# Cross-attention and routed experts on one core: the opening of the attention stage re-cut, and the row statistics spread over six units

## What is computed

```
q = (layernorm(x) @ w_q.T + b_q) * 32**-0.5
k = ctx @ w_k.T + b_k ;  v = ctx @ w_v.T + b_v
scores = q.k per head + attn_bias ; masked keys get -max
out = softmax(scores) @ v
x = x + out @ w_out.T + b_out
y = layernorm(x)
# 32 prototypes: distance to each, softmax, best two kept and renormalised
x = x + sum over the two best experts: A[e] @ (B[e] @ y) + bias[e]
```

## Time and profile before

| | |
|---|---|
| median of 3 runs | 939.32 us (937.33 to 940.16) |
| the profiled execution, its own time | 940.71 us |
| its span, first to last instruction | 939.0 us |
| TensorE busy in the span | 874.2 us (93%) |
| VectorE, ScalarE, GpSimd busy | 621.2, 499.9, 200.4 us |
| mean granted TensorE clock | 0.978 of full speed |

### The profile page before, as it was taken

How to read it: one execution, slowest core, us unless ns; L and a number is a source line. 1 busy time by engine, 2 the same in 40 slices (tenths; PEclk the granted TensorE clock), 3 DMA queues, 4 the chain that set the end, 5 groups by cost and what they waited for, 6 DMA issues and landing times. The chain is left out here.

```text
span 939.0 us, 20884 instructions
## 1 busy us (share of the span) xinstructions
PE 874.2 (93%) x8016; PEld 761.9 (81%) x8016; DVE 621.2 (66%) x1452; ACT 499.9 (53%) x1061; POOL 200.4 (21%) x245
## 2 busy tenths in 40 slices
PE   7789999999999999999999999999989778999996
PEld 6678987898889788978987898889777567878884
DVE  5646675667667766766676667666677465666663
ACT  4226655565556565656655565556577334444431
POOL 1251022002201121220022002210084213333200
PEclk9889999999999999999999999999999979999999
DMA  7795654554565556655654554475565211222101
GB/s 247 220 221 132 161 142 119 143 155 119 137 166 150 134 142 146 166 131 136 152 150 120 143 154 120 104 177 139 131 163 121 67 40 40 62 65 68 59 20 39
DMA packets 79402, 119.77 MB, mean 128 GB/s; under 512 B 8469, under 2 KB 58749, under 8 KB 79314
## 3 DMA queue, kind: packets, MB, share of 16 engines
q1 hardware_dynamic: 76818, 109.91, 45.9%
q0 software_dynamic: 2496, 8.65, 3.0%
HBM read 79.25 MB, written 39.28 MB: 126 GB/s over the span
## 5 line engine op out<-in xcount | busy, mean ns | idle before, releaser
L568 ACT ACTIVATE score_sb<-score_sb,neg_max 112x750 f32<-112x750 f32 x256 | 236.0, 922 | 94.4 <-DVE neg_max L696 93.6
L696 DVE CUSTOM_DVE_ANT_0 score_sb<-score_ps,neg_bias 112x750 f32<-112x750 f32 x256 | 239.5, 935 | 65.3 <-PE score_ps L858 63.4
L867 PE MATMUL prob_ps<-ident,score_sb 112*125 112x112 f32 x1536 | 254.7, 275 | 18.9 <-ACT score_sb L568 8.5
L867 PEld LDWEIGHTS prob_ps<-ident,score_sb 112*125 112x125 f32 x1536 | 226.5, 189 | 51.5 <-issue 13.3
L577 ACT ACTIVATE probs_sb<-prob_ps 125x336 f32<-125x336 f32 x256 | 114.8, 449 | 181.5 <-PE prob_ps L867 179.9
L706 DVE COPY probs_sb<-prob_ps 125x336 f32<-125x336 f32 x256 | 129.6, 506 | 120.5 <-PE prob_ps L867 118.3
L465 POOL COPY rsum_wide<-rsum 112x256 f32<-112x256 f32 x32 | 12.8, 399 | 460.6 <-DVE rsum L715 460.5
L854 PE MATMUL score_ps<-k_st,q_st 97*112 97x512 f32 x256 | 108.4, 424 | 0.0
L813 PE MATMUL acc<-ctx_hi,w_hi 128*128 128x376 f32 (+1 forms) x256 | 93.9, 367 | 7.5 <-DVE ctx_lo L731 6.7
L813 PE MATMUL acc<-ctx_hi,w_lo 128*128 128x376 f32 (+1 forms) x256 | 91.8, 358 | 0.0
L813 PE MATMUL acc<-ctx_lo,w_hi 128*128 128x376 f32 (+1 forms) x256 | 91.5, 357 | 0.0
(11 more groups left out here) (163 smaller groups left out, 1510.8 us busy)
## 6 DMA issues: line engine op xcount, KB each, us to landing
k_st<-k_parts SPq DMA_DIRECT2D x96, 375.0 KB
q_st<-q_parts SPq DMA_DIRECT2D x96, 112.0 KB
ctx_raw<-in_ctx_t SPq DMA_DIRECT2D x14, 752.0 KB, 7.0
k_parts<-k_hi SPq DMA_DIRECT2D x30, 188.0 KB, 1.9
k_parts<-k_lo SPq DMA_DIRECT2D x30, 188.0 KB, 2.3
k_parts<-k_hi SPq DMA_DIRECT2D x30, 187.0 KB, 2.9
k_parts<-k_lo SPq DMA_DIRECT2D x30, 187.0 KB, 4.3
xb<-in_x SPq DMA_DIRECT2D x8, 448.0 KB, 4.1
```

The source lines that it names most:

```text
L568: nc.scalar.activation(scores[:, w % NSC, :], scores[:, w % NSC, :], ACT.Exp, bias=neg_max[:, w % UB:w % UB + 1], scale=-1.0, accum_out=su ...
L696: nc.vector.tensor_tensor_reduce(out=scores[:, w % NSC, :], in0=score_ps[:, at:at + S], in1=neg_bias[:, w // HG % TC, :], scale=1.0, scala ...
L867: last = nc.tensor.transpose(prob_ps[j][0:SW, s * TW:(s + 1) * TW], scores[:, w % NSC, (BT * j + s) * SW:(BT * j + s + 1) * SW], ident[0:T ...
```

## The change

- **Query weights.** GpSimd's three operations are gone. The weights come in four DMAs of a quarter each. ScalarE makes the high part of each quarter straight from the stage with scale -SCALE (`high_queries`, behind the high evictions of tiles 3, 4, 4 and 5), VectorE the low part by one scalar_tensor_tensor (`low_queries`, behind the low evictions of tiles 4, 5, 5 and 6).
- **Value weights.** The quarters' high parts stand together (one before the eviction of tile 7, three behind it), the low parts behind tiles 7 (three) and 8 (one). Before, they stood one by one behind tiles 6 to 9.
- **Statistics of batch 0:** `newton` and `normalise` stand behind tile 3 (before: tile 4). Batch 1: statistics behind tile 12 (before: 10), normalisation behind 13 (before: 12). `turn_x(c)` waits only for its own half.
- **Bias:** negated by VectorE behind tiles 10 and 11; its DMA is issued after the stores of key tiles 2 and 3. Those two stores now stand behind the mask, value bias and value weights.
- **First scores.** TensorE does `score(0)` before the last value tile, `score(1)` after 8 of its 12 steps, then the last 4. VectorE does `add(0)` and `add(1)` before the eviction of that tile.
- **Unit loop.** Statistics at u = 20, 21 and 22, the root at 23, Newton at 25, normalisation at 26 and 27. `last` is 31. At u = 3 and 4 the wait for x or for the attention output stands behind `turn(w, 0)`.

```diff
-    busy, burst, last = 1000, 1500, UB - 2
+    busy, burst, last = 1000, 1500, UB - 1
...
-            eng.dma_start(w_stage[0], w_in_t[:, 0:E].rearrange("(k p) o -> p k o", p=P)).then_inc(wq_loaded, 16)
-            for n in range(NG):
+            for k in range(KT):
+                eng.dma_start(w_stage[0][:, k, :], w_in_t[k * P:(k + 1) * P, 0:E]).then_inc(wq_loaded[k], 16)
+            for n in range(2):
                 store_tile(0, n)
...
+            for n in range(2, NG):
+                store_tile(0, n)
+            eng.dma_start(neg_bias[:, :, :], bias.rearrange("(c t) s -> t c s", c=TC)).then_inc(bias_loaded, 16)
...
             root(0)
-            eng.wait_ge(wq_loaded, 16)
-            eng.tensor_scalar(w_stage[0], w_stage[0], -SCALE, 0.0, ALU.mult, ALU.add).then_inc(wq_step, 1)
-            eng.wait_ge(wq_step, 1)
-            eng.tensor_scalar(w_hi[0][:, :, :], w_stage[0], 1.0, 0.0, ALU.mult, ALU.add).then_inc(wq_step, 1)
-            eng.wait_ge(wq_step, 2)
-            eng.tensor_tensor(w_lo[0][:, :, :], w_stage[0], w_hi[0][:, :, :].bitcast(F32), ALU.subtract)\
...
-            eng.wait_ge(bias_loaded, 16)
-            for c in range(TC):
-                eng.tensor_scalar(neg_bias[:, c, :], neg_bias[:, c, :], -1.0, BIAS_MAX, ALU.mult, ALU.min)\
...
-                if b < B - 2 and u == 21:
+                if b < B - 2 and u == 23:
                     root(b + 2)
...
+            def high_queries(k):
+                eng.wait_ge(wq_loaded[k], 16)
+                nc.scalar.activation(w_hi[0][:, k, :], w_stage[0][:, k, :], ACT.Copy, scale=-SCALE)\
+                    .then_inc(wq_hi_ready, 1)
...
+                if n == 3:
+                    high_queries(0)
+                if n == 4:
+                    high_queries(1)
+                    high_queries(2)
+                if n == 5:
+                    high_queries(3)
+                if n == 2 * NG - 1:
+                    for k in range(1, KT):
+                        high_values(k)
...
+            def low_queries(k):
+                eng.wait_ge(wq_hi_ready, k + 1)
+                nc.vector.scalar_tensor_tensor(w_lo[0][:, k, :], w_stage[0][:, k, :], -SCALE,
+                                               w_hi[0][:, k, :].bitcast(F32), ALU.mult, ALU.subtract)\
...
+                if n == NT - 1:
+                    eng.wait_ge(bias_ready, TC)
+                    eng.wait_ge(wq_ready, KT)
+                    eng.wait_ge(mask_stored, 16)
+                    add(0)
+                    add(1)
                 low_tile(0, n)
...
+                if n in (2, 2 * NG + 4):
+                    b = n // NG // 2
+                    for c in range(TC):
+                        x_stats(b, c)
+                    x_variance(b)
+                if n in (3, 2 * NG + 5):
+                    b = n // NG // 2
+                    newton(b)
+                    for c in range(TC):
+                        normalise(b, c)
...
-                if u == 20 and b < B - 2:
-                    x_stats(b + 2)
-                if u == 24 and b < B - 2:
-                    normalise(b + 2)
+                if b < B - 2:
+                    if u in (20, 21):
+                        x_stats(b + 2, u - 20)
+                    if u == 22:
+                        x_variance(b + 2)
+                    if u == 25:
+                        newton(b + 2)
+                    if u in (26, 27):
+                        normalise(b + 2, u - 26)
...
-            project_steps(0, before_x, tile_ends(0)[NT - 1])
+            last_value = tile_ends(0)[NT - 2]
+            project_steps(0, before_x, last_value)
             eng.wait_ge(ones_ready, 2)
             score(0)
+            project_steps(0, last_value, last_value + 2 * KT)
             score(1)
+            project_steps(0, last_value + 2 * KT, last_value + 3 * KT)
             for w in range(UNITS + 2):
                 b, u = divmod(w, UB)
                 m = CUTS[b + 1][u] if b + 1 < B else (0,) * 4
+                if w < UNITS:
+                    turn(w, 0)
                 if b + 1 < B and u in X_AT:
...
-                if w < UNITS:
-                    turn(w, 0)
```

More of the change, by code:

```diff
@@ L267, in weave @@
         wk_loaded = [sem(f"wk_loaded{k}") for k in range(KT)]
-        wq_loaded = sem("wq_loaded")
+        wq_loaded = [sem(f"wq_loaded{k}") for k in range(KT)]
         wv_loaded = [sem(f"wv_loaded{k}") for k in range(KT)]
@@ L277, in weave @@
         wv_ready = sem("wv_ready")
-        wq_step = sem("wq_step")
+        wq_hi_ready = sem("wq_hi_ready")
+        wq_ready = sem("wq_ready")
         bias_col_loaded = sem("bias_col_loaded")
@@ L405, in _ @@
                 store_tile(0, n)
-            eng.dma_start(neg_bias[:, :, :], bias.rearrange("(c t) s -> t c s", c=TC)).then_inc(bias_loaded, 16)
             eng.wait_ge(mask_stored, 16)
@@ L583, in sums_out, with high_values @@
                 nc.scalar.activation(rsum_t[:, :], out_ps[:, 256:256 + T], ACT.Copy).then_inc(rsum_t_ready, 1)
+            def high_queries(k):
+                eng.wait_ge(wq_loaded[k], 16)
+                nc.scalar.activation(w_hi[0][:, k, :], w_stage[0][:, k, :], ACT.Copy, scale=-SCALE)\
+                    .then_inc(wq_hi_ready, 1)
+            def high_values(k):
+                eng.wait_ge(wv_loaded[k], 16)
+                nc.scalar.activation(w_hi[2][:, k, :], w_stage[2][:, k, :], ACT.Copy).then_inc(wv_hi_ready, 1)
             for k in range(KT):
@@ L594, in _ @@
                         high_x(0, c, prob_ps[c])
+                    high_values(0)
                     eng.wait_ge(nbq_ready, 1)
@@ L662, in low_x, with x_stats, x_variance @@
                     .then_inc(xt_ready, 1)
-            def x_stats(b):
+            def x_stats(b, c):
                 eng.wait_ge(x_loaded, 16 * (b + 1))
-                for c in range(TC):
-                    nc.vector.bn_stats(stats[:, c, :], x_in[:, c, :]).then_inc(stat_step, 1)
+                nc.vector.bn_stats(stats[:, c, :], x_in[:, c, :]).then_inc(stat_step, 1)
+            def x_variance(b):
                 eng.wait_ge(stat_step, 2 * TC * b + TC)
@@ L684, in normalise, with low_values, negate_bias @@
                 nc.vector.tensor_tensor(nwt[:, 3, :], nwt[:, 2, :], rstd[:, :], ALU.mult).then_inc(newton_step, 1)
+            def normalise(b, c):
                 eng.wait_ge(newton_step, 4 * b + 4)
[L686 to L689, removed]
+                nc.vector.tensor_scalar(x_in[:, c, :], x_in[:, c, :], mv[:, c, 0:1], nwt[:, 3, c:c + 1],
+                                        ALU.subtract, ALU.mult).then_inc(xn_ready, 1)
+            def low_queries(k):
+                eng.wait_ge(wq_hi_ready, k + 1)
+                nc.vector.scalar_tensor_tensor(w_lo[0][:, k, :], w_stage[0][:, k, :], -SCALE,
+                                               w_hi[0][:, k, :].bitcast(F32), ALU.mult, ALU.subtract)\
+                    .then_inc(wq_ready, 1)
+            def low_values(k):
+                eng.wait_ge(wv_hi_ready, k + 1)
+                nc.vector.tensor_tensor(w_lo[2][:, k, :], w_stage[2][:, k, :], w_hi[2][:, k, :].bitcast(F32),
+                                        ALU.subtract).then_inc(wv_ready, 1)
+            def negate_bias(c):
+                eng.wait_ge(bias_loaded, 16)
+                nc.vector.tensor_scalar(neg_bias[:, c, :], neg_bias[:, c, :], -1.0, BIAS_MAX, ALU.mult, ALU.min)\
+                    .then_inc(bias_ready, 1)
             def add(w):
@@ L748, in _ @@
                             .then_inc(ctx_ready[1], 1)
[L749 to L766, removed]
+                if n in (2, 2 * NG + 4):
[8 more added lines that the diff above has]
+                        normalise(b, c)
+                if n == 4:
+                    low_queries(0)
+                if n == 5:
+                    low_queries(1)
+                    low_queries(2)
+                if n == 6:
+                    low_queries(3)
+                if n == 2 * NG - 1:
+                    for k in range(KT - 1):
+                        low_values(k)
+                if n == 2 * NG:
+                    low_values(KT - 1)
+                if n in (2 * NG + 2, 2 * NG + 3):
+                    negate_bias(n - 2 * NG - 2)
             for w in range(UNITS + 3):
@@ L836, in turn_x @@
             def turn_x(b, c, dst):
-                eng.wait_ge(xn_ready, b + 1)
+                eng.wait_ge(xn_ready, TC * b + c + 1)
                 for k in range(KT):
```

11 lines of the change are left out of this document (2 added, 9 removed).

## The result

The changed kernel takes 936.17 us in the median of 11 runs (lowest 930.73), the kernel before 940.16 in 11 runs beside it. The ratio is 0.9943 with a 95% interval of 0.9923 to 0.9964: 0.6% faster, where 2.3% was forecast, and outside the range. One of the 11 runs of the changed kernel took 2890.63 us and is left out of the ratio. The profiled execution took 936.17 us, its span 934.5 (before: 940.71 and 939.0).

A forecast was written before the change was run, and what follows sets the result against it. TensorE was taken as the bound, so its idle and half-clock time could be won. The parts' 5.9 + 5.7 + 9.5 = 21.1 us off 940.71 gave 919.6, 918 as a median; own range 912 to 924, overall 911 to 929.

The forecast's parts named there:

- First part, query weights and statistics: Opening: GpSimd's 8.3 us go, query tiles begin at about 29.25 instead of 35.17, 5.9 us earlier; bounds 5.1 to 7.6.
- The stall at tile 6: Opening: VectorE's eviction of tile 4 ends at 23.9, tile 6 wants it at 22.8; a new stall of 1.1 us.
- lower bound: Opening: key tile 2's store seen landed at 26.7, ScalarE wants it at 25.95; costs 0.8 and leaves 5.1 us.
- Second part, first scores: From value tile 0 to the loop at full pace: Q + 22.6 instead of Q + 28.27, 5.7 us gained; bounds 3.7 to 7.1.
- with no hole longer than about 1.4 us: First scores: with holes no longer than this, the full clock was expected, so loop pace at Q + 22.6.
- Third part, the unit loop: Loop: spread statistics, moved waits and 31 units give 9.1 us, plus 0.4 for the clock; bounds 2 and 14.
- Spreading the statistics: Loop: splitting statistics and normalisation over units takes 0.4 of TensorE's 0.6 us wait, six times, 2.5 us.
- Waits behind `turn(w, 0)`: Loop, u = 3 and 4: 0.25 us of transposes run during the waits; 1.5 for attention output, 2.0 for x.
- 31 units: Loop, batch end: only u = 31 left bare; 0.94 us of waits becomes 0.5, at `add(33)`; 3.1 us over seven.
- no effect: Rival, chance 0.02: something else, such as the key loads, sets the loop's start; time stays at 939.
- The loop gives nothing: Rival, chance 0.17: the six pieces and last value eviction open waits as large as those they close; 927.7 us.
- The opening's tail is kept: Rival, chance 0.13: VectorE behind tile 13 waits out GpSimd instructions, clock falls, second part gives nothing; 923.9 us.

The follow-up runs named there:

- e10: e3 with the query weights again on GpSimd as three whole instructions; 926.91 us, ratio 0.9844 to the kernel before.
- e3: The changed kernel (31 units) with the next group's key loads issued one unit later, u % 8 = 7 in place of 6; 917.09 us, ratio 0.9748.
- e5: e3 with the statistics together again: at u = 20, root at 21, Newton and both normalisations at u = 24; 926.27 us, ratio 0.9816.
- e2: The kernel before with only the projection steps spread over 31 units; 945.89 us, ratio 1.0064.
- e8: e3 with the first two scores and their additions again behind the last value tile; 918.54 us, ratio 0.9739.
- e1: The changed kernel with projection steps spread over 30 units again (last = UB - 2); 921.33 us, ratio 0.9793.
- e7: The changed kernel with 30 units and the key loads at u % 8 = 7, both edits of e1 and e3; 920.66 us, ratio 0.9765.
- e4: The opening as changed, the unit loop as in the kernel before (30 units, old statistics and wait places); 927.89 us, ratio 0.9877.
- e9: As e1 (30 units), with the key loads early at u % 8 = 4, in front of key tile 5's store; 959.49 us, ratio 1.0190.

## Why the prediction was wrong

**First part, query weights and statistics: cause and sum right, the sum in part by luck.** Forecast: query tiles from 29.25; measured 29.42. The stall at tile 6 was 0.69 (forecast 1.1): the normalisations took 1.01 where the 1.58 of the earlier trace rows was assumed, a row that was itself slowed by GpSimd's bias. But the late store of key tile 2, which the forecast put only in its lower bound, did occur. ScalarE evicted key tile 6 at 26.39, near the 26.7 of that bound, and TensorE's wait before the queries was 0.98 (forecast 0.6). The shorter stall paid for the late store. No run takes that store order back. e10 shows the cause of the first hole. The Trainium skill (SBUF — State Buffer, "Who interferes with whom") says that VectorE and GpSimd share a port pair that is an exclusive lock. e10's rows agree: a 2-column tensor_tensor took 1.77 us there, ending with a GpSimd instruction of 1.91 us, where it takes 0.16 in e3's loop. So do the stretched Newton instructions of e5.

**Second part, first scores: the sum right, two terms wrong.** Forecast for the first score Q + 14.7 and for the first key step Q + 19.2, where Q is the start of value tile 0, 34.85; measured Q + 14.4 and Q + 18.8. The key loads had no such margin as the forecast gave them (Q + 13.3): from the first issue at 38.95 to the score that waited for them they took 10.3 us, not 7.7, and the score waits 0.20 us for them here and 0.67 in e3. They were issued 1.5 us earlier than taken, which hid it. The lead at the batch 1 marker is 11.5 us, where both parts together were forecast at 11.6. e2, with the opening of the kernel before, has that marker at 70.18, not 71.58, with a half-clock stretch from 63 to 67 us, not from 61 to 69; so the lead is uncertain by about 1.5 us. e8 shows that the interleaving of the scores carries only about 1.5 of it. The rest comes from the earlier split and from a clock that does not fall. The forecast expected full clock "with no hole longer than about 1.4 us". That held in the opening, but no run shows 1.4 us as a limit: in the loop the clock fell behind waits of 1.55 to 1.79 us and not behind others of 1.54 to 1.66.

**Third part, the unit loop: the step that failed.** The step was "`last` = 31: only u = 31 is left bare; unit 30 gets 13 value steps", priced at a gain of 3.1 us. It followed TensorE and VectorE to the end of the batch and not the other tiles that the new share moves, nor SyncE's queue. Key tile 5 moved from unit 20 to unit 22 and its store behind the key loads. The wait of 1.5 to 1.8 us took the whole gain of the loop (a step at full clock takes 88.05 us, as before), and the clock fell in four steps of seven. Forecast 9.5 us faster, measured 7 slower (4.5 in all, less 11.5): the six marked steps together are 3.1 us longer than before, the seventh is another 3.5 (from the last mark to VectorE's last attention output of that batch pass 87.6 us against 84.1), and the rest of the execution 0.4. e1, e2, e3 and e7 together show that the share and the place of the loads make it together and neither alone.

Without the collision (e3) a step is 88.06 - 86.18 = 1.88 us shorter. That holds for the six marked steps, 11.3 us. The seventh, in which nothing is normalised, gains nothing that can be told (84.2 against 84.1 us between the same two points). So the loop is worth some 11 us, where 9.5 was forecast, and 1.6 more in the profiled execution, as the clock does not fall in the first step. e3 takes 917.09 us, ratio 0.9748, where the forecast of 918 is 0.9773; it is another kernel than the one forecast, and its terms were off in size:
- Spreading the statistics: 0.4 of 0.6 us was taken; e5 against e3 gives 1.48 per batch. The forecast left out that the move to u = 25 also takes the Newton instructions away from GpSimd's split (2.2 against 0.64 us of VectorE). Moreover the listed wait is only 0.9 per batch in e5: from the start of the last matmul before it to that of the second group of transposes behind it pass 3.27 us in e5 and 1.86 in e3, 1.41 more.
- Waits behind `turn(w, 0)`: 3.5 us taken, 0.73 per batch measured, 4.4 over the six batches and near 5 over seven.
- 31 units: 0.44 per batch taken, 0.32 measured (e3 against e1 and e7). The wait forecast for `add(33)` is not there; one of 0.32 at u = 20 is, behind the eviction of key tile 4.

These three make 2.53, more than the 1.88 of all together: they are not independent. With 30 units the first two are worth 88.05 - 86.50 = 1.55 together (e4 against e1), with 31 units 1.48 + 0.73 = 2.21. With 31 units key tile 7 ends in unit 24, where the undivided normalisation stands, and with 30 units in unit 23. The wait for the copy is 0.92 us in e5 and 0.93 in e2 (31 units), against 0.61 in e4 and in the kernel before (30). So the larger share has a second cost, which the spreading hides.

The rivals: by the number *no effect* (939) came nearest to 936.17, by chance, as a gain and a loss nearly cancel. *The loop gives nothing* was right that something in the loop eats the gain, but by mechanism it was not it, since the spread pieces and the last value eviction opened no waits as large as those they closed (e1, e3), and the loop gave less than nothing. *The opening's tail is kept* did not happen: VectorE's normalisations behind tile 13 took 1.96 us and the clock stayed up. A rival for the DMA queue in the loop was missing.

What stays open: why the clock fell in four of seven batch steps after waits of nearly the same length, what kept it up behind the first scores, what the late store of key tile 2 costs, and how much of e9's 6 us per batch belongs to each store.

## What to carry to other kernels

When work is shared out anew over a loop, list for every tile the unit in which it ends before and after, and read off which DMA its store now stands behind in the order of issue, and who wants its buffer next; with two staging buffers the tile after next pays. A store that frees a buffer belongs in front of a bulk load that has a unit to spare: here moving the loads by one unit turned 0.6% into 2.5%. A chain of small instructions on VectorE belongs in a unit in which GpSimd is idle: here that took it from 2.2 to 0.64 us. Price a wait from start to start of the instructions around it, as the listed idle time can be too small.

## What the runs showed of the hardware

Two DMAs of 187 KB each, which landed in 1.9 to 2.1 us in the kernel before and in e3, took 6.7 and 7.6 us when the first was issued 3.6 us behind the first of seven loads of 1.5 MB in all. Three of VectorE's four Newton instructions of 2 columns, 0.15 to 0.16 us each in e3, took 0.78, 0.43 and 0.84 beside GpSimd's split in e5. A TensorE wait of 1.55 us was followed by 3.4 us at 1.2 GHz and a batch longer by 1.6; the same kernel's batches with waits of 1.54 to 1.66 us and no fall took 88.0 to 88.1. Two waits of 1.06 and 0.77 us close together, in e8, left the clock at 2.4 GHz, while the kernel before fell after 1.06, 0.76 and 0.80.
